# The order in which several waits of one instruction are written, in a four-stage chain of cross-attention layers

## The reference

```python
x = L0(x, ctx)          # channel attention: softmax(q k) v, one head, + x
x = L1(x, ctx, masks)   # self attention, cross attention (16 heads of 16), gelu MLP, layernorms
x = L2(ctx, x, mask)    # 32 latents attend to 256 + 32 rows (16 heads), rms norm, gelu MLP
x = L3(x, ctx, ctx)     # two cross attentions of 16 heads of 128, then a gelu MLP
```

```python
qh = (q_in @ wq + bq).reshape(b, q_len, H, K)          # H = 16, K = 128
kh = (kv_in @ wk + bk).reshape(b, t, H, K)             # vh alike
kh = concatenate([kh, bias_k], axis=1)                 # one learned key, vh: one learned value
weights = softmax(einsum('bqhk,bthk->bhqt', qh, kh) / sqrt(K), axis=-1)
ctx = einsum('bhqt,bthk->bqhk', weights, vh).reshape(b, q_len, H * K)
return ctx @ wo + bo
```

## Time and profile before

| | us |
|---|---|
| median of 3 runs | 2092.25 |
| the runs | 2090.29, 2092.25, 2092.61 |
| profiled execution | 2090.38 |
| its span, first to last instruction | 2088.3 |
| mean granted clock of TensorE | 0.98 |

### The profile page before, as it was taken

How to read it: one execution, slowest core, us unless ns; L and a number is a source line. 1 busy time by engine, 2 the same in 40 slices (tenths; PEclk the granted TensorE clock), 3 DMA queues, 4 the chain that set the end, 5 groups by cost and what they waited for, 6 DMA issues and landing times.

```text
span 2088.3 us, 43180 instructions
## 1 busy us (share of the span) xinstructions
PE 1927.6 (92%) x14880; PEld 1680.0 (80%) x14880; DVE 1272.4 (61%) x4143; ACT 1182.8 (57%) x3878; POOL 678.2 (32%) x613
## 2 busy tenths in 40 slices
PE   4678899999999899888999999999999999999989
PEld 3457677787878777667999999999799999999878
DVE  2577797979797865455555555556555555555653
ACT  2466888788787876545444444444644444444631
POOL 1333443434444443533222222223322222213452
PEclk8789999999999999999999999999999999999999
DMA  7000000000000000001000000000000000000100
GB/s 264 8 10 7 6 7 7 12 2 7 1 7 2 4 2 2 22 1 44 26 16 25 20 25 15 25 15 26 11 26 26 15 25 20 15 20 0 41 11 31
DMA packets 24635, 44.35 MB, mean 21 GB/s; under 512 B 2336, under 2 KB 12064, under 8 KB 23584
## 3 DMA queue, kind: packets, MB, share of 16 engines
q1 hardware_dynamic: 23328, 34.13, 5.5%
q10 hardware_dynamic: 1152, 8.26, 1.0%
HBM read 40.28 MB, written 2.10 MB: 20 GB/s over the span
## 4 chain that ended last, share of the span: by engine, by line
PE 49%; DVE 2%; issue 1%; ACT 1%; POOL 1%; ACTq 0%; DVEq 0%; POOLq 0%
PE general L1969 33%; PE o_psum L2026 6%; PE scores L2008 5%; PE pT_psum L2093 3%; PE scores L2148 1%; PE pT_psum L2148 1%; PE o_psum L2148 1%; ACT probs L1632 0%; PE general L1980 0%; POOL probs L1533 0%; DVE guess L1310 0%; ACT kT L1615 0%; ACT xhat L1605 0%; DVE row_stats L1765 0%; DVE X L1814 0%
## 5 line engine op out<-in xcount | busy, mean ns | idle before, releaser
L557 POOL TENSOR_TENSOR probs<-probs,rsums 128x512 f32<-128x512 f32 (+1 forms) x288 | 283.9, 998 | 484.9 <-DVE rsums L787 484.2
L1533 POOL TENSOR_TENSOR probs<-probs,rsums 128x512 f32<-128x512 f32 x128 | 133.4, 1042 | 721.9 <-DVE rsums L1796 721.9
L610 ACT ACTIVATE probs<-negated,negmax 128x128 f32<-128x128 f32 (+1 forms) x768 | 325.4, 430 | 12.0 <-DVE negmax L778 11.8
L1640 ACT COPY probsT<-pT_psum 128x512 f32<-128x512 f32 x128 | 75.0, 586 | 280.7 <-PE pT_psum L2093 280.7
L1105 PE MATMUL pT_psum<-ident,probs 128*128 128x128 f32 x1072 | 175.0, 285 | 53.9 <-ACT probsT L618 26.4
L1105 PEld LDWEIGHTS pT_psum<-ident,probs 128*128 128x128 f32 x1072 | 124.4, 144 | 108.0 <-issue 59.4
L1969 PE MATMUL general<-hT,w_qk 128*128 128x512 f32 x768 | 206.9, 405 | 1.1 <-ACT kT L1615 0.8
L1969 PE MATMUL general<-ctxT,w_qk 128*128 128x512 f32 x750 | 192.2, 393 | 2.9 <-DVEq L222 2.9
L1969 PE MATMUL general<-w_o,oT 128*128 128x256 f32 x1536 | 193.7, 281 | 0.9 <-ACT oT L1648 0.9
L1648 ACT ACTIVATE oT<-o_psum,hcols 128x512 fp32r<-128x512 f32 x128 | 88.1, 689 | 187.3 <-PE o_psum L2026 187.3
L1632 ACT ACTIVATE probs<-scores,negmax 128x128 f32<-128x128 f32 x512 | 180.5, 370 | 24.0 <-DVE negmax L1788 24.0
(11 more groups left out here) (199 smaller groups left out, 3915.4 us busy)
## 6 DMA issues: line engine op xcount, KB each, us to landing
raw_qk<-w_qk_dram SPq DMA_DIRECT2D x32, 256.0 KB, 2.9
weights_a<-weights_a_dram ACTq DMA_DIRECT2D x2, 2048.0 KB, 17.8
raw_v<-w_v_dram SPq DMA_DIRECT2D x16, 256.0 KB, 2.7
raw_vrows<-vrows_dram SPq DMA_DIRECT2D x16, 256.0 KB, 3.4
raw_o<-w_o_dram SPq DMA_DIRECT2D x16, 256.0 KB, 2.7
weights_a<-weights_a_dram ACTq DMA_DIRECT2D x3, 1024.0 KB, 9.7
X<-x_dram SPq DMA_DIRECT2D x8, 256.0 KB, 7.6
ctx_in<-ctx_dram SPq DMA_DIRECT2D x8, 256.0 KB, 2.8
```

What stands on the lines that cost most here:

```text
L557: nc.gpsimd.tensor_tensor(pr, pr, rsums[:, n % 4, 0:segs].unsqueeze(2).broadcast_to([P, segs, width(kind) // segs]), ALU.mult).then_inc(s[ ...
L610: last = nc.scalar.activation(probs[:, n % PROBS, i * wide:(i + 1) * wide], src[:, i * wide:(i + 1) * wide], ACT.Exp, scale=1.0 if kind == ...
L1533: nc.gpsimd.tensor_tensor(pr, pr, rsums[:, t % 2, :].unsqueeze(2).broadcast_to([P, NB, P]), ALU.mult).then_inc(s["probs_ready"], 1)
```

## The change

The waits of five functions of stage 3 and of six of stages 0 to 2 are written in another order; no wait is added or left out, no count differs, and the instructions and their order on every engine stay as they are. In each function the wait for the producer that is expected last is now the last one before the instruction: `max_ready` for the exponentials, `pT_ready` for the copies of the transposed probabilities, `exp_done` for the sums, `probs_ready` for the transposes, `pT_copied` for the values. The whole diff:

```diff
--- before.py
+++ after.py
@@ -602,9 +602,9 @@
                 def exps(kind, g, u):
                     n, segs = index(kind, g, u), segments(kind)
                     wide = width(kind) // segs
-                    act.wait_ge(s["max_ready"], n + 1)
                     wait_count(act, s["pT_ready"], n - PROBS + 1)
                     wait_count(act, s["rsum_ready"], n - 3)
+                    act.wait_ge(s["max_ready"], n + 1)
                     for i in range(segs):
                         src = score_bank(n) if kind == "chan" else negated[:, n % 4, :]
                         last = nc.scalar.activation(probs[:, n % PROBS, i * wide:(i + 1) * wide], src[:, i * wide:(i + 1) * wide],
@@ -613,8 +613,8 @@
 
                 def copy_pT(kind, g, u):
                     n = index(kind, g, u)
+                    wait_count(act, s["pv_done"], n - 3)
                     act.wait_ge(s["pT_ready"], n + 1)
-                    wait_count(act, s["pv_done"], n - 3)
                     nc.scalar.copy(probsT[:, n % 4, 0:width(kind)], turned(kind, g, u)[:, 0:width(kind)]).then_inc(s["pT_copied_act"], 1)
 
                 def copy_o(kind, g, u):
@@ -782,14 +782,14 @@
 
                 def rsum(kind, g, u):
                     n, segs = index(kind, g, u), segments(kind)
+                    wait_count(dve, s["probs_ready"], n - 3)
                     dve.wait_ge(s["exp_done"], n + 1)
-                    wait_count(dve, s["probs_ready"], n - 3)
                     nc.vector.reciprocal(rsums[:, n % 4, 0:segs], sums[:, n % 4, 0:segs]).then_inc(s["rsum_ready"], 1)
 
                 def copy_pT(kind, g, u):
                     n = index(kind, g, u)
+                    wait_count(dve, s["pv_done"], n - 3)
                     dve.wait_ge(s["pT_ready"], n + 1)
-                    wait_count(dve, s["pv_done"], n - 3)
                     nc.vector.tensor_copy(probsT[:, n % 4, 0:width(kind)], turned(kind, g, u)[:, 0:width(kind)]).then_inc(s["pT_copied_dve"], 1)
 
                 def chan_residual(g, b):
@@ -1094,13 +1094,13 @@
 
                 def transpose_probs(kind, g, u):
                     n = index(kind, g, u)
-                    pe.wait_ge(s["probs_ready"], n + 1)
                     if apart(kind, g, u) and u == UNITS_OF["lat"] // 2 + 1:
 
                         earlier = [use for use in USES_A[:USES_A.index(("lat_o", g))] if uses[use][0] == 1]
                         wait_copied(pe, *earlier[-1])
                     else:
                         wait_pT_copied(pe, n - 2 if apart(kind, g, u - 1) or apart(kind, g, u) else n - 1)
+                    pe.wait_ge(s["probs_ready"], n + 1)
                     for j in range(width(kind) // P):
                         last = nc.tensor.transpose(turned(kind, g, u)[:, j * P:(j + 1) * P], probs[:, n % PROBS, j * P:(j + 1) * P], ident[:, :])
                     last.then_inc(s["pT_ready"], 1)
@@ -1112,13 +1112,13 @@
                     units = BLOCK_UNITS[kind]
                     n = index(kind, g, u)
                     c, b, _ = unit_parts(kind, u)
-                    for e in range(units - 2, units):
-                        wait_pT_copied(pe, n + e)
                     wait_block_read(pe, block_of(kind, g, u) - 1)
                     out = o_psum
                     if u == 0:
                         for name in {"lat": ("lat_v", "ctx_v")}.get(kind, (kind + "_v",)):
                             wait_copied(pe, name, g)
+                    for e in range(units - 2, units):
+                        wait_pT_copied(pe, n + e)
                     if kind == "chan":
                         for e in range(2):
                             for m in range(2):
@@ -1625,18 +1625,16 @@
                     nc.scalar.activation(qT[:, head, quarter(t % G)], src[:, :], ACT.Identity, bias=hcols[:, bass.ds(at, 1)]).then_inc(freed, 1)
 
                 def exps(n, t):
+                    act.wait_ge(s["pT_ready"], n if t > 0 else n + 1)
                     act.wait_ge(s["max_ready"], n + 2)
-
-                    act.wait_ge(s["pT_ready"], n if t > 0 else n + 1)
                     for b in range(NB):
                         nc.scalar.activation(probs[:, t % 2, b * P:(b + 1) * P], scores[t % 2][:, b * P:(b + 1) * P], ACT.Exp,
                                              bias=negmax[:, t % 2, b:b + 1], scale=SCALE3, accum_out=sums[:, t % 2, b:b + 1])
                     nc.scalar.activation(learned[:, t % 2, :], negmax[:, t % 2, :], ACT.Exp).then_inc(s["exp_done"], 1)
 
                 def copy_pT(n):
+                    act.wait_ge(s["o_ready"], n + 1)
                     act.wait_ge(s["pT_ready"], n + 2)
-
-                    act.wait_ge(s["o_ready"], n + 1)
                     nc.scalar.copy(probsT[:, :], pT_psum[:, :]).then_inc(s["pT_copied"], 1)
 
                 def copy_o(a, i, n, t):
@@ -1788,9 +1786,8 @@
                     nc.vector.tensor_scalar(negmax[:, t % 2, :], rawmax[:, t % 2, :], 0.0, SCALE3, ALU.min, ALU.mult).then_inc(s["max_ready"], 1)
 
                 def rsum(n, t):
+                    dve.wait_ge(s["probs_ready"], n if t > 0 else n + 1)
                     dve.wait_ge(s["exp_done"], n + 2)
-
-                    dve.wait_ge(s["probs_ready"], n if t > 0 else n + 1)
                     nc.vector.tensor_tensor(totals[:, t % 2, :], sums[:, t % 2, :], learned[:, t % 2, :], ALU.add).then_inc(s["rsum_step"], 1)
                     dve.wait_ge(s["rsum_step"], n + 2)
                     nc.vector.reciprocal(rsums[:, t % 2, :], totals[:, t % 2, :]).then_inc(s["rsum_ready"], 1)
@@ -2011,7 +2008,6 @@
                 def weigh_values(n, t, a, section, loop):
                     head = t // G
 
-                    pe.wait_ge(s["pT_copied"], n + 2)
                     if head == 0:
                         for half in range(2):
                             if section == "lead":
@@ -2022,6 +2018,7 @@
                             else:
                                 wait_copied(pe, section, a, loop, ("v", t, half))
                     pe.wait_ge(s["o_lo"], n + 1)
+                    pe.wait_ge(s["pT_copied"], n + 2)
                     for j in range(NB):
                         last = nc.tensor.matmul(o_psum[:, j * P:(j + 1) * P], v[:, head, (t % G) * NB + j, :], probsT[:, j * P:(j + 1) * P], start=True, stop=True)
                     last.then_inc(s["o_ready"], 1)
@@ -2086,9 +2083,8 @@
                                 if key[2] == 0:
                                     pe.wait_ge(s["o_hi"], n + 1)
                                 output(section, a, loop, key[1], key[2], (lambda: pe.wait_ge(s["o_lo"], n + 1)) if key[2] == 0 else None)
+                        pe.wait_ge(s["pT_copied"], n + 1)
                         pe.wait_ge(s["probs_ready"], n + 2)
-
-                        pe.wait_ge(s["pT_copied"], n + 1)
                         for j in range(NB):
                             last = nc.tensor.transpose(pT_psum[:, j * P:(j + 1) * P], probs[:, t % 2, j * P:(j + 1) * P], ident[:, :])
                         last.then_inc(s["pT_ready"], 1)
```

## The result

The changed kernel takes 2109.59 us (median of 7 runs, 2100.28 to 2111.07) against 2092.49 (7 runs, 2090.29 to 2096.44). The ratio is 1.0073 with a 95% interval of 1.0061 to 1.0084: slower by some 15 us. The direction was forecast; the size, +6.3 with an upper end of 2106, was not. A second set beside later experiments gave 2106.38 against 2092.33, 1.0062 (1.0049 to 1.0075). The seven times fall into two groups: four of 2109.6 to 2111.1 at a mean granted clock of 0.977, and three of 2100.3 to 2104.2 at 0.978 to 0.981; the profiled execution, 2110.2, is of the first.

What follows compares the result with a forecast made beforehand. PE was taken to bound stage 3's loops, with about 6% idle in stages 0-2. Terms 5.4 - 1.9 + 0.8 + 0.7 + 1.3 + 0 = +6.3 us gave a median of 2098.5 (+0.30%), range 2091 to 2106.

Steps and rivals of the forecast that it cites:

- Which wait rides: All reordered functions: the wait written first rides on the instruction, the rest become sequencer instructions; nothing below changes without it.
- Head 0 of the loops: Stage 3 loops, 48 steps: copy wait leaves the register operation, -0.04 each, -1.9 us.
- Head 1 of the loops and the unrolled steps: Stage 3, 36 loop and about 24 unrolled steps: values start 0.09 later each, 60 x 0.09 = +5.4 us.
- the price of 0.09: Stage 3 head 1 and similar unrolled steps: the values' first matmul starts 0.09 us later in each.
- The eighth step: Eighth step of each loop pass in stage 3: load waits for POOL without margin, 12 x 0.06 = +0.7 us.
- DVE's place: Stage 3 sums' late wait on a sequencer instruction: taken as nothing; at 0.06 it would add 2.0, kept in the upper end.
- The late unrolled steps: About 5 unrolled stage 3 steps with the copy already late: both prices in full, 5 x 0.15 = +0.8 us.
- the sum of 0: Stages 0-2: transposes' copy waits -1.7, POOL waits +2.6, others nothing; whole put at 0, ends -1.7 and +2.6.
- Rival 1: Whole kernel: terms cancel if ACT's place costs nothing or half of 0.06; 2089 to 2094, nearer 2093; chance 0.23.
- ACT's place: Stage 3 copies: late wait on a sequencer instruction starts the copy 0.06 later; ends 0 and 0.09.
- Rival 2: Whole kernel: the wait written last rides, so head 0 gaps close and transposes gain; 9.6 faster, 2082.7; chance 0.10.
- Rival 3: Stage 3 copies: ACT's place is dear, 0.12 over the present 0.03, from a 0.21 delay; +15.1, 2107; chance 0.15.

Runs made afterwards that it cites:

- stage 3's parts: Three kernels with new order in stage 3 only for copies; values; or exponentials, sums and transposes, against the kernel before: +5.9, 0 and +2.9 us.
- the kernel with the wait off the register operation: Kernel before, but a semaphore increment in the loops' head 0 values takes up the bank waits before the copy's wait: 2086.27 against 2093.35, ratio 0.9965.
- the stage 3 half: Only the five functions of stage 3 have the new order, stages 0-2 as before: 2099.8 against 2092.2 for the kernel before, ratio 1.0044.
- the fill: 34 unread identity transposes on PE around the stage 2/3 seam: changed kernel 2100.57 with, 2106.38 without; stages 0-2 alone changed 2095.02 with, 2098.83 without.
- the copies alone: Only stage 3's copies of the transposed probabilities have the new order, against the kernel before: 2098.03 against 2092.2, ratio 1.0028.
- the values alone: Only the weighing of the values in stage 3 has the new order, against the kernel before: 2092.56, ratio 1.0000.

## Why the prediction was wrong in size and right in kind

**Which wait rides: right.** The rows of the late waits became sequencer instructions, 128 or 116 of 128; the sum of stage 3's parts and the kernel with the wait off the register operation (-7.3) follow from it.

**Head 0 of the loops: right.** -0.04 a step was forecast; from 1.03 to 0.99. Summed over the 48 steps in the trace of the stage 3 half: -2.0 us, -1.9 forecast.

**Head 1 of the loops and the unrolled steps: the gap right, the price too small.** 0.99 from scores to values was forecast and measured. The step that failed is the price of 0.09: it ended at the first matmul. A load that comes late also takes away the lead that the loads have over the matmuls, and the group of eight grows by 0.03 (1.10 to 1.13). That is 0.12 a step to the end of the group, and 60 x 0.03 = 1.8 us missing from the sum. It was to be read in rows 6 and 8, where the two groups have these lengths; I read only their starts.

**The eighth step: the step that failed is DVE's place, put at nothing.** The sums come 0.07 later. The load comes 0.06 later as forecast, but that delay doesn't reach the first transpose; 0.03 of it comes back in the length of the group. In the trace of the exponentials, sums and transposes alone the eighth step is 0.09 longer: 12 x 0.09 = 1.1 instead of 0.7. The forecast had kept 2.0 for DVE in its upper end.

**The late unrolled steps: +0.8 that did not come.** Four unrolled steps of before have the values 0.99 to 1.08 after the scores; in the trace of the stage 3 half they have 0.99 to 1.06.

With the group's 1.8, the eighth step's 0.4 and without the 0.8, 6.3 becomes 7.7 for stage 3; measured +9.2, with an interval from 6.1 to 12.1. The 1.5 between them are not assigned.

**Stages 0-2: the step that failed is the sum of 0.** There are two causes. First, I priced the copies on the 57 handovers to the transposes and left the exponentials and sums at nothing because of cover seen in stage 3. By themselves the copies cost 2.5 and the others 2.3 (the latter not clear of zero), against 1.0 gained by the transposes, for whose edit the forecast's terms give 57 x -0.09 + 2.6 = -2.5. The three sum to +3.8 by their ratios, and the traces of all three contain the fall at the seam. Second, nothing in the sum stood for the clock. By the runs with and without the fill, the seam accounts for 2.9 of the 5.2, not clear of the noise, and in the whole change for 5.8, which is. So it is shown that the clock has a part, but not how the 5.2 divides between handovers and clock. Rows 1 shows 1.00 in the loops, and I never read the windows around the seam, where an idle stretch of 2.9 us stands.

**The rivals.** Rival 1 (it cancels) falls with the copies alone at +5.9: ACT's place costs 0.06, as taken. Rival 2 (the wait written last rides) falls with the rows above and with the values alone at 0. Rival 3 named a time near the measured one, 2107, but by a mechanism that the trace of after rules out: the copies start 0.06 later, not 0.12, and its 0.21 belongs to steps with register operations.

**The start of the profile.** The 0.72 between 60 and 125 us makes the profiled execution after some 5 us longer at 125 us than before. In the second profile of the same kernel the clock there is 0.77 and the trace is 0.7 us ahead at 125. Of the eleven profiles with changed stages 0-2 three have 0.71 to 0.74 there (after, the copies, the exponentials and sums) and eight 0.76 or 0.77; all seven with the old stages have 0.77 or 0.78. So it was seen with the change alone, but not in every execution, and why it falls in some stays open.

## What to carry to other kernels

Before reordering waits, look in the trace which of them appear as sequencer rows: a wait without a row rides on the instruction, and that place belongs to the producer that comes last. Here the order in the code is the reverse of what one would think: the first written rides, unless a register operation between the waits takes it. Price a late weight load by the length of the whole group behind it, not by the gap in front. And when time is gained ahead of an idle stretch on TensorE, read the granted clock behind it before counting the gain.

## What the runs showed of the hardware

Where the late wait stood on a sequencer instruction instead of on the instruction itself, a copy on ACT began 0.06 us later, the sums on DVE 0.07 and a weight load 0.06. Behind such a load a group of eight matmuls began 0.04 later and ended 0.06 later; a group of four transposes began no later and ended 0.03 later. The copy and the values together make the 0.12 of a step. Behind a semaphore increment that took up the wait, an ACT copy began 0.02 later than behind a plain wait instruction. With a register operation carrying the wait it is 0.24 us from copy to matmul, against 0.14 behind a sequencer instruction and 0.11 with the wait riding and no gap left. And 34 transposes whose results nobody reads, put around an idle stretch of 2.9 us, made the changed kernel 5.8 us faster, with the granted clock there going from 0.94 to 1.00.
